# Two 128-row tiles in each step of a two-layer graph attention kernel, and the first layer's V bias moved behind the heads

## The chip, the cores and the metric

One core of one Trainium2 chip. The metric is the device time of one execution in microseconds. The kernel before took 1067.73 us, the median of three runs (1065.7 to 1071.74).

## What is computed

x is (128, 64, 384): 128 graphs of 64 nodes. Both layers are attention with 12 heads of 32, with a residual and a layer norm:

```
layer 0: q = x@Wq+bq; k = x@Wk+bk; v = x@Wv+bv          (bv not zero)
         s = q k^T / sqrt(32) + beta*adj, and -9e15 where adj <= 0
         x = layernorm(x + softmax(s) v)
layer 1: q = x@Wq.T; k = x@Wk.T; v = x@Wv.T + bv
         s = q k^T / sqrt(384) + adj; a row that is all zero gives 0
         x = layernorm(x + (softmax(s) v)@Wo.T + bo)
```

Everything is float32. The rows of a softmax sum to one, so softmax(s)(v + bv) = softmax(s) v + bv: the changed kernel uses this in layer 0.

## The kernel before

**Chunks, tiles, turns.** The 8192 rows are 16 chunks of four tiles (128 rows, two graphs, each). A turn is one chunk in one layer. `ORDER` has 32 turns: three of layer 0, then layer 1 and layer 0 by turns, at last three of layer 1. A turn has four steps, one for each tile. In a step each engine runs through a list that is written out by hand, and each engine executes its list in order; semaphores join them.

**Units.** The projections are made a chunk ahead of their use, as "units": three of q and three of k (128 output features by the 512 rows of the chunk) and four of V (128 rows by 384 features). A float32 product is split into three: each operand has a high part (rounded to fp32r) and a low part (the rest), and low x high, high x low and high x high are summed over three slices of 128, so nine matmuls a unit (L374). Units alternate between the two banks of `ps_u`; a unit waits until its bank's last user has been evicted. `units_of_step` deals the ten units of a turn over its steps: q0, k0, k1; then q1, k2; then q2, V0, V1; then V2, V3. The first of a step is "early", the others are "late".

**A step.** With `cur` the tile attended now, `prev` the one before it, `last` the one before that, and `turned` the tile two turns ahead:

- TensorE (tensor block): scores of `cur` into `ps_s` (L392, 48 matmuls of 32x64); the early unit; the result of `last` (L498: three transposes in layer 0; L374 into `ps_h`: the Wo product in layer 1); the transposes of `turned`'s rows into `ps_h` where it is of layer 1 (L410); the transposes of `prev`'s probabilities into `ps_s` (L464, six); the late units; the heads of `prev` (L486, 48 matmuls).
- VectorE: bias added to the scores (L675, two instructions), row maxima (L684; in layer 1 also of the absolute values, L683), early V eviction, the residual of `last` (z L752, then statistics), xt_lo of `turned` (L693, layer 1 only), the row sums of the exponentials (L716) and their reciprocals, late V evictions with the bias (L709), o_lo of `prev` (L733, layer 1), and at the end of a layer-0 turn the next chunk's bias (L643, L645).
- GpSimd: the maxima subtracted (`shift`, L806), bo added to `turned`'s rows (L822) or, in layer 0, its xt_lo (L832), the normalisation of `last` (L846, L852), the probabilities scaled (`scale`, L812).
- ScalarE: early eviction of a q or k unit (L585 to L591), xt_hi of `turned` (L553), the turned probabilities copied out (L559), the exponential of `cur` (L597), the late evictions, the heads copied out (L605).
- SyncE: the stores of layer 1 and the loads of x, of its transpose and of adj.

Of the kernel before, what the change touches and what calls it, by code (L numbers as in the profile page):

```python
# [12 lines left out]
P = 128  # L13
# [7 lines left out]
TILES = 4  # L21

# [15 lines left out]
Step = namedtuple("Step", "phase t cur prev last done turned units")  # L38
# [19 lines left out]

def schedule():
    steps = []  # L60
    attended = {}
    for phase in range(-1, N_TURNS + 1):
        for t in range(TILES if phase < N_TURNS else 3):
            s = TILES * phase + t
            if 0 <= phase < N_TURNS:
                attended[s] = (*ORDER[phase], t)
            turned = (*ORDER[phase + 2], t) if phase + 2 < N_TURNS else None
            units = units_of_step(phase, t) if phase < N_TURNS else []
            steps.append(Step(phase, t, attended.get(s), attended.get(s - 1), attended.get(s - 2),
                              attended.get(s - 3), turned, units))  # L70
    return steps


STEPS = schedule()

# [10 lines left out]
UNIT_ORDER = [u for s in STEPS for u in s.units]  # L86
UNIT_NO = {u: n + 1 for n, u in enumerate(UNIT_ORDER)}
QK_NO = {u: n + 1 for n, u in enumerate(u for u in UNIT_ORDER if u[2] != "v")}
V_NO = {u: n + 1 for n, u in enumerate(u for u in UNIT_ORDER if u[2] == "v")}
TURN_ORDER = [s.turned for s in STEPS if s.turned]  # L90
# [22 lines left out]
def two_gnn_layers_kernel(  # L113
# [33 lines left out]
    with ExitStack() as ctx:  # L147
# [25 lines left out]
        adj1 = [sb(f"adj1_{p}", [P, GC, NODES]) for p in range(2)]  # L173

        probs = [sb(f"probs{p}", [P, PAIRS, GT, NODES]) for p in range(2)]
        probs_t = sb("probs_t", [P, PAIRS, P])
        o_t = sb("o_t", [P, KT, P])
        o_hi = sb("o_hi", [P, KT, P], F32R)
        o_lo = sb("o_lo", [P, KT, P], F32R)
        z = [sb(f"z{p}", [P, D]) for p in range(2)]  # L180
        bv_rows = [sb(f"bv_rows{l}", [P, D]) for l in range(2)]
# [7 lines left out]
        row_max = [sb(f"row_max{p}", [P, PAIRS * GT]) for p in range(2)]  # L189
        row_abs = [sb(f"row_abs{p}", [P, PAIRS * GT]) for p in range(2)]  # L190
        row_sum = [sb(f"row_sum{p}", [P, PAIRS * GT]) for p in range(2)]
        row_inv = [sb(f"row_inv{p}", [P, PAIRS * GT]) for p in range(2)]
        row_fac = [sb(f"row_fac{p}", [P, PAIRS * GT]) for p in range(2)]
# [4 lines left out]
        w_stage = sb("w_stage", [P, KT, D])  # L198
# [8 lines left out]
        row_in = sem("row_in")  # L207
# [20 lines left out]
        xt_made = sem("xt_made")  # L228
# [16 lines left out]
        v_ready = sem("v_ready")  # L245
# [17 lines left out]
        def as_weight(home):  # L263
            flat = home[:].rearrange("p a b n -> p (a b n)") if len(home.shape) == 4 \
                else home[:].rearrange("p a n -> p (a n)")
# [3 lines left out]
                 "q1": as_weight(x1[1]), "k1": as_weight(x1[2]), "v1": as_weight(x_in[1]), "o1": w_stage[:]}  # L269
# [16 lines left out]
        def _(sp):  # L286
# [26 lines left out]
            def load_adj1(c):  # L313
                if c >= 2:
                    sp.wait_ge(biased, at((1, c - 2, TILES - 1)) + 1)
                load_adj(c, adj1[c % 2], adj1_loaded[c % 2])
# [10 lines left out]
            sp.dma_start(k_bias[:], bk0).then_inc(small_in, 16)  # L327
            sp.dma_start(beta_col[:], beta.rearrange("(o n) -> o n", o=1).partition_broadcast(P))\
# [7 lines left out]
            load_row(bv_rows[0], bv0, row_in)  # L336
# [4 lines left out]
            load_row(bv_rows[1], bv1, rows_in)  # L341
# [4 lines left out]
            for s in STEPS:  # L346
                if s.done and s.done[0] == 1:
                    _, c, t = s.done
                    sp.wait_ge(normed, at(s.done) + 1)
                    sp.dma_start(out_rows[c * CT + t * P:c * CT + (t + 1) * P, :], z[t % 2][:])\  # L350
                        .then_inc(stored[t % 2], 16)

                of = s.phase + 1
                if s.t == 0 and of < N_TURNS and ORDER[of][0] == 0 and 2 <= ORDER[of][1] < CHUNKS - 1:
                    load_xt(ORDER[of][1] + 1)
                if s.t == 1 and 0 <= s.phase < N_TURNS and ORDER[s.phase][0] == 0:
                    if ORDER[s.phase][1] < CHUNKS - 1:
                        load_adj0(ORDER[s.phase][1] + 1)
                if s.t == 2 and s.phase == 0:
                    load_x(1)  # L360
                if s.t == 2 and 1 <= s.phase <= N_TURNS and ORDER[s.phase - 1][0] == 0:
                    if ORDER[s.phase - 1][1] + 2 < CHUNKS:
                        load_x(ORDER[s.phase - 1][1] + 2)
                if s.t == 1 and 0 <= s.phase < N_TURNS - 1 and ORDER[s.phase + 1][0] == 1:
                    load_adj1(ORDER[s.phase + 1][1])
            for p in range(2):
# [3 lines left out]
        def _(pe):  # L370
# [7 lines left out]
            def scores(tile):  # L378
                layer, c, t = tile
                p = home((layer, c))  # L380
                if t == 0:
                    pe.wait_ge(qk_ready, last_qk((layer, c)))
                if at(tile) > 0:
                    pe.wait_ge(biased, at(tile))
                if at(tile) > 1:
                    pe.wait_ge(probs_t_ready, at(tile) - 1)
                for g in range(KT):
                    for b in range(GT):
                        for hh in range(HG):
# [3 lines left out]
                                ps_s[side * NODES:(side + 1) * NODES, half_of * GT + b, g * NODES:(g + 1) * NODES],  # L393
# [4 lines left out]
            def heads_read(tile):  # L398
                pe.wait_ge(o_t_ready, at(tile) + 1)
                if tile[0] == 1:  # L400
                    pe.wait_ge(o_lo_ready, second_no(tile))

            def turn_activations(tile, last_heads):
                layer, c, t = tile
                if layer == 0:
                    return
                pe.wait_ge(normed, at((0, c, t)) + 1)
                heads_read(last_heads)
                for g in range(KT):
                    last = nc.tensor.transpose(ps_h[:, 1, g * P:(g + 1) * P], x1[c % 3][:, t, g * P:(g + 1) * P],  # L410
                                               ident[:])
                last.then_inc(xt_made, 1)

            def make_unit(unit):
                layer, c, kind, n = unit
                p, no = home((layer, c)), UNIT_NO[unit]
                if no > 2:
                    freed = UNIT_ORDER[no - 3]
                    if freed[2] == "v" and freed[:2] == ORDER[-1]:
                        pe.wait_ge(last_v_copied, freed[3] + 1)  # L420
                    elif freed[2] == "v":
                        pe.wait_ge(v_ready, V_NO[freed])
                    else:
                        pe.wait_ge(qk_ready, QK_NO[freed])
# [14 lines left out]
                elif no == 1:  # L439
                    for g in range(KT):  # L440
                        pe.wait_ge(first_lo, 2 * g + 2)
                        cols = slice(n * P, (n + 1) * P)
                        nc.tensor.matmul(ps_u[:, bank, :], w_lo[w][:, g, cols], xt_hi[p][:, g, :],
                                         start=(g == 0), stop=False)
                        nc.tensor.matmul(ps_u[:, bank, :], w_hi[w][:, g, cols], xt_lo[p][:, g, :],
                                         start=False, stop=False)
                        last = nc.tensor.matmul(ps_u[:, bank, :], w_hi[w][:, g, cols], xt_hi[p][:, g, :],
# [455 lines left out]
```

## Time and profile before

| | before |
|---|---|
| median of 3 runs | 1067.73 us |
| the profiled execution's own time | 1066.61 us |
| its span | 1064.8 us |
| TensorE matmuls | 1035.8 us, 97% of the span |
| VectorE | 793.6 us, 75% |
| GpSimd | 788.6 us, 74% |
| ScalarE | 451.0 us, 42% |
| mean granted TensorE clock | 0.996 |

How to read it: PE is TensorE's matmuls, PEld its weight loads, DVE VectorE, ACT ScalarE, POOL GpSimd, SP SyncE. L374 is line 374 of the kernel. The start times in a timeline are more telling for matmuls than their lengths, since the next starts before the last has drained. `x18` is a count of instructions that follow each other.

### The profile page before, as it was taken

The page shows a single profiled execution, that of the slowest core. Times are in us where ns is not written, and L with a number is a line of the kernel's source. Part 1 is how long each engine was busy: PE and PEld are TensorE (multiplying, and loading weights), DVE is VectorE, ACT ScalarE, POOL GpSimd, SP SyncE. Part 2 cuts the span into 40 slices and gives each one's busy share as a digit, 9 for nine tenths or more (in the row PEclk, how much of TensorE's full clock was granted, in tenths as well). Part 3 has the DMA queues.
Part 4 walks back from the last instruction along what each step waited for, and adds up shares of the span by engine and source line. Part 5 has one row for each costly group of instructions (what it writes and reads, how often), then busy time and mean ns, then how long its engine had stood idle before and what let it go on. Part 6 is the DMA issues. An engine that isn't in the chain of part 4 may idle for free.

```text
span 1064.8 us, 38493 instructions
## 1 busy us (share of the span) xinstructions
PE 1035.8 (97%) x16896; PEld 898.1 (84%) x16896; DVE 793.6 (75%) x1578; ACT 451.0 (42%) x717; POOL 788.6 (74%) x646
## 2 busy tenths in 40 slices
PE   6999999999999999999999999999999999999985
PEld 5888888888888888888888888888888888888874
DVE  3587886868778687786868778687786868877884
ACT  4454434444344443444445344443434444444332
POOL 1588777778687786877778777777877867777676
PEclk9999999999999999999999999999999999999998
DMA  6421112112111121111211021121111210010100
GB/s 205 142 71 52 34 44 66 40 44 62 40 44 39 44 62 44 40 46 39 67 44 52 33 59 39 44 62 44 39 47 36 62 44 10 17 37 10 35 32 31
DMA packets 61750, 53.33 MB, mean 50 GB/s; under 512 B 35984, under 2 KB 55440, under 8 KB 61584
## 3 DMA queue, kind: packets, MB, share of 16 engines
q1 hardware_dynamic: 60752, 49.69, 15.9%
q8 instruction: 134, 2.20, 0.9%
q10 hardware_dynamic: 832, 1.18, 0.3%
q14 instruction: 32, 0.26, 0.1%
HBM read 38.28 MB, written 12.58 MB: 48 GB/s over the span
## 4 chain that ended last, share of the span: by engine, by line
PE 89%; DVE 3%; POOL 3%; issue 2%; DMA 1%; ACT 1%; POOLq 0%; SPq 0%; DVEq 0%
PE ps_u L374 53%; PE ps_h L374 9%; PE ps_s L392 8%; PE ps_s L464 8%; PE ps_h L486 7%; PE ps_h L410 2%; PE ps_h L498 2%; POOL probs L806 1%; DMA xt_in<-in_x_t 1%; DVE row_sum L716 1%; ACT probs L597 1%; DVE probs L675 1%; DVE row_max L684 1%; POOL probs L812 0%; POOL xt_lo L832 0%
## 5 line engine op out<-in xcount | busy, mean ns | idle before, releaser
L806 POOL TENSOR_TENSOR probs<-probs,row_max 128x768 f32<-128x768 f32 x128 | 193.2, 1510 | 223.2 <-DVE row_max L684 223.2
L812 POOL TENSOR_TENSOR probs<-probs,row_inv 128x768 f32<-128x768 f32 x128 | 193.2, 1509 | 2.8 <-DVE row_inv L720 2.5
L716 DVE TENSOR_REDUCE row_sum<-probs 128x12 f32<-128x768 f32 x128 | 122.0, 953 | 68.0 <-ACT probs L597 68.0
L559 ACT COPY probs_t<-ps_s 128x768 f32<-128x768 f32 x128 | 102.8, 803 | 109.9 <-PE ps_s L464 109.8
L374 PE MATMUL ps_u<-w_hi_v,xt_lo 128*128 128x384 f32 x384 | 137.7, 359 | 0.0
L374 PE MATMUL ps_u<-w_hi_v,xt_hi 128*128 128x384 f32 x384 | 129.4, 337 | 0.0
L374 PE MATMUL ps_u<-w_lo_v,xt_hi 128*128 128x384 f32 x384 | 129.1, 336 | 0.0
L684 DVE TENSOR_REDUCE row_max<-probs 128x12 f32<-128x768 f32 x128 | 121.4, 948 | 2.2
L374 PE MATMUL ps_u<-xt_hi,w_lo_q 128*128 128x512 f32 x285 | 121.6, 427 | 0.0
L597 ACT ACTIVATE probs<-probs 128x768 f32<-128x768 f32 x128 | 108.6, 849 | 28.9 <-POOL probs L806 27.0
L374 PE MATMUL ps_u<-xt_hi,w_lo_k 128*128 128x512 f32 x288 | 118.2, 410 | 0.9 <-ACT q_sb L585 0.9
L374 PE MATMUL ps_u<-xt_hi,w_hi_k 128*128 128x512 f32 x288 | 113.0, 392 | 0.0
L374 PE MATMUL ps_u<-xt_lo,w_hi_k 128*128 128x512 f32 x288 | 112.2, 390 | 0.0
L374 PE MATMUL ps_u<-xt_lo,w_hi_q 128*128 128x512 f32 x285 | 111.8, 392 | 0.0
L374 PE MATMUL ps_u<-xt_hi,w_hi_q 128*128 128x512 f32 x285 | 111.8, 392 | 0.0
L852 POOL TENSOR_SCALAR x<-z,mean_var,rstd 128x384 f32<-128x384 f32 x64 | 106.1, 1658 | 6.7
L852 POOL TENSOR_SCALAR z<-z,mean_var,rstd 128x384 f32<-128x384 f32 x64 | 105.9, 1655 | 6.7
L486 PEld LDWEIGHTS ps_h<-probs_t,v_sb 64*32 64x32 f32 x6144 | 72.3, 105 | 41.8 <-issue 40.6
L464 PE MATMUL ps_s<-ident,probs 128*128 128x128 f32 x768 | 105.9, 274 | 1.2 <-DVE probs L675 1.1
L392 PE MATMUL ps_s<-k_sb,q_sb 32*64 32x64 f32 x6144 | 99.8, 231 | 1.2 <-ACT k_sb L587 0.8
L486 PE MATMUL ps_h<-probs_t,v_sb 64*32 64x64 f32 x6144 | 92.6, 223 | 2.5 <-DVE xt_lo L693 1.4
L392 PEld LDWEIGHTS ps_s<-k_sb,q_sb 32*64 32x64 f32 x6144 | 82.2, 131 | 13.6 <-ACT k_sb L587 1.2
(80 smaller groups left out, 2102.6 us busy)
## 6 DMA issues: line engine op xcount, KB each, us to landing
x_in<-in_x SPq DMA_DIRECT2D x16, 768.0 KB, 4.6
out<-z SPq DMA_DIRECT2D x64, 192.0 KB, 1.9
xt_in<-in_x_t SPq DMA_DIRECT2D x15, 768.0 KB, 4.7
adj<-in_adj SPq DMA_DIRECT2D x64, 128.0 KB, 3.0
xt_in<-in_x_t SPq DMA_DIRECT2D x3, 256.0 KB, 4.4
q_sb<-in_wq ACTq DMA_DIRECT2D x3, 192.0 KB, 4.6
k_sb<-in_wk ACTq DMA_DIRECT2D x1, 576.0 KB, 7.4
v_sb<-in_wv SPq DMA_DIRECT2D x1, 576.0 KB, 7.3
```

The lines of the kernel that those rows point to most:

```text
L374: last = nc.tensor.matmul(dst, a(g), b(g), start=(g == 0 and n == 0), stop=(g == KT - 1 and n == 2))
L392: last = nc.tensor.matmul(ps_s[side * NODES:(side + 1) * NODES, half_of * GT + b, g * NODES:(g + 1) * NODES], q_sb[p][rows, g, GT * t + b, :],
L410: last = nc.tensor.transpose(ps_h[:, 1, g * P:(g + 1) * P], x1[c % 3][:, t, g * P:(g + 1) * P], ident[:])
L464: last = nc.tensor.transpose(ps_s[:, i // KT, (i % KT) * P:(i % KT + 1) * P], probs[t % 2][:, i, :, :], ident[:])
L486: last = nc.tensor.matmul(ps_h[hh * HD:(hh + 1) * HD, b, g * NODES:(g + 1) * NODES], v_sb[p][keys, t, h * HD:(h + 1) * HD], probs_t[keys, ...
L559: nc.scalar.copy(probs_t[:].rearrange("p (a i) n -> p a (i n)", a=2), ps_s[:, 0:2, 0:KT * P]).then_inc(probs_t_ready, 1)
L597: nc.scalar.activation(e, e, ACT.Exp).then_inc(exp_ready, 1)
L684: nc.vector.tensor_reduce(row_max[t % 2][:], rows, AX_X, ALU.max).then_inc(max_ready, 1)
L716: nc.vector.reduce_sum(row_sum[p][:], probs[p][:].rearrange("p i b k -> p (i b) k"), AX_X)\
L806: nc.gpsimd.tensor_tensor(s, s, over_keys(row_max[p]), ALU.subtract).then_inc(shifted, 1)
L812: nc.gpsimd.tensor_tensor(s, s, over_keys(row_inv[p]), ALU.mult).then_inc(probs_ready, 1)
L852: nc.gpsimd.tensor_scalar(dst, z[t % 2][:], mean_var[t % 2][:, 0:1], rstd[t % 2][:], ALU.subtract, ALU.mult).then_inc(normed, 1)
```

## The change

Turns 2 to 27 have two steps of two tiles; turns 0, 1 and 28 to 31 keep four steps of one. In a paired step each engine takes both tiles: TensorE the scores of both one behind the other, then one early unit, both results, both tiles' columns, both turned probabilities, four late units, both heads. `cur`, `prev` and `last` are now tuples, so in a paired turn `last` is the pair two steps back, which belongs to the turn before. Four buffers of probabilities (and of row maxima, sums and so on) take the place of two, two of turned probabilities the place of one; `o_t`, `o_hi` and `o_lo` hold two tiles.

The transposes of layer 1's rows ("x" units, `columns`) go through the banks of `ps_u`, between the early and the late units, so that both banks of `ps_h` serve results.

Layer 0's V is copied out by ScalarE with no bias; its bias is added when the heads are copied out, as a column, in three ScalarE instructions a step. Layer 1's V stays on VectorE.

At the start TensorE runs ten products on the identity; the first two units are made together, slice by slice, high parts first. The first scores wait for each slice's q and k alone. SyncE's stores stand behind the step's loads, one step earlier than before. Wo is staged in the space of `adj1`, whose first load therefore waits for Wo's low part. The bias of V in layer 0 is loaded as a column beside the other small constants.

The core of the diff (`j` is the place of a tile in its step):

```diff
+def slots(phase):
+    if 2 <= phase <= N_TURNS - 5:
+        return [(0, 1), (2, 3)]
+    return [(0,), (1,), (2,), (3,)] if phase < N_TURNS else [(0,), (1,)]
...
+def columns(s):
+    return [(*tile[:2], "x", tile[2]) for tile in s.turned if tile[0] == 1]
...
+UNIT_ORDER = [u for s in STEPS for u in early(s) + columns(s) + late(s)]
...
         # TensorE
+            warm_up()
+            first_units()
             for s in STEPS:
-                if s.cur:
-                    scores(s.cur)
+                for j, tile in enumerate(s.cur):
+                    scores(tile, j, s)
                 for unit in early(s):
...
+                for j, tile in enumerate(s.last):
+                    result(tile, j, s)
+                for unit in columns(s):
+                    turn_activations(unit)
+                for j, tile in enumerate(s.prev):
+                    turn_probs(tile, j, s)
                 for unit in late(s):
...
+                for j, tile in enumerate(s.prev):
+                    heads(tile, j, s)
...
         # ScalarE
             def unit_out(unit):
-                if kind == "v" and (layer, c) != ORDER[-1]:
+                if kind == "v" and layer == 1 and (layer, c) != ORDER[-1]:
                     return
...
+            def heads_out(tiles):
...
+                if layer == 1:
+                    nc.scalar.copy(dst, src).then_inc(o_t_ready, len(tiles))
+                    return
+                for g in range(KT):
+                    done = nc.scalar.activation(dst[:, g::KT, :, :], src[:, g::KT, :, :], ACT.Identity,
+                                                bias=bv_col[:, g:g + 1])
+                done.then_inc(o_t_ready, len(tiles))
...
+                for unit in early(s):
+                    unit_out(unit)
...
+                for j, tile in enumerate(s.prev):
+                    probs_out(tile, j, s)
+                for tile in s.cur[:1]:
+                    exponentials(tile)
+                for unit in late(s)[:1]:
                     unit_out(unit)
+                for tile in s.cur[1:]:
+                    exponentials(tile)
+                for unit in late(s)[1:]:
+                    unit_out(unit)
...
         # VectorE
+                for j, tile in enumerate(s.cur):
+                    add_bias(tile, j, s)
+                for tile in s.cur[:1]:
+                    maxima(tile)
...
+                if s.phase >= 0:
+                    for tile in s.turned:
+                        activations_lo(tile)
+                for j in range(2):
+                    for tile in s.last[j:j + 1]:
+                        residual(tile, j)
+                    if len(s.ts) == 2:
+                        for unit in late(s)[j:j + 1]:
+                            unit_out(unit)
+                for tile in s.cur[1:]:
+                    maxima(tile)
+                for tile in s.cur[:1]:
+                    sums(tile)
+                for unit in late(s)[2 if len(s.ts) == 2 else 0:]:
+                    unit_out(unit)
+                for tile in s.cur[1:]:
+                    sums(tile)
...
         # GpSimd
+                for tile in s.cur[:1]:
+                    shift(tile)
...
+                for tile in s.cur[1:]:
+                    shift(tile)
+                for j in range(2):
+                    for tile in s.last[j:j + 1]:
+                        inverse_deviation(tile)
+                        normalise(tile)
+                    for tile in s.cur[j:j + 1]:
+                        scale(tile)
```

## Rows read from the trace of the kernel before

**Rows 1.** the page's first part: busy us (share of the span) x instructions of each engine.

```profile
span 1064.8 us, 38493 instructions
...
PE 1035.8 (97%) x16896; PEld 898.1 (84%) x16896; DVE 793.6 (75%) x1578; ACT 451.0 (42%) x717; POOL 788.6 (74%) x646
```

**Rows 2.** the chain of waits: start in us, length, engine, tile, line, count.

```profile
430.72 3.13 PE ps_u L374 x18
...
495.09 3.13 PE ps_u L374 x18
```

**Rows 3.** timeline of TensorE, one layer-0 step: start us, length us, engine, line.

```profile
501.51 0.82 PE L464 MATMUL ps_s<-ident,probs 128*128 128x128 f32 x6
...
502.08 0.42 PE L374 MATMUL ps_u<-w_hi_v,xt_lo 128*128 128x384 f32 x1
...
503.40 0.34 PE L374 MATMUL ps_u<-w_lo_v,xt_hi 128*128 128x384 f32 x1
...
503.58 0.34 PE L374 MATMUL ps_u<-w_hi_v,xt_hi 128*128 128x384 f32 x1
503.85 0.56 PEld L486 LDWEIGHTS ps_h<-probs_t,v_sb 64*32 64x32 f32 x48 [0.26 <-issue]
...
504.51 0.78 PE L392 MATMUL ps_s<-k_sb,q_sb 32*64 32x64 f32 x48
...
505.22 0.50 PE L374 MATMUL ps_u<-xt_hi,w_lo_q 128*128 128x512 f32 x1
...
505.78 0.40 PE L374 MATMUL ps_u<-xt_hi,w_hi_q 128*128 128x512 f32 x1
...
507.40 0.49 PE L498 MATMUL ps_h<-ident,o_t 128*128 128x128 f32 x3
```

**Rows 4.** timeline of the other engines, the end of that turn and one layer-1 step.

```profile
505.23 0.49 DVE L709 TENSOR_TENSOR v_sb<-ps_u,bv_rows 128x384 f32<-128x384 f32 x1
...
505.64 0.41 DVE L643 TENSOR_SCALAR bias<-adj 128x512 f32<-128x512 f32 x1
...
506.76 1.01 DVE L675 TENSOR_TENSOR probs<-ps_s,adj 128x384 f32<-128x384 f32 x2
...
507.81 0.95 DVE L683 TENSOR_REDUCE row_abs<-probs 128x12 f32<-128x768 f32 x1
...
509.54 0.55 DVE L752 TENSOR_TENSOR z<-ps_h,x_in 128x384 f32<-128x384 f32 x1
...
509.70 1.48 POOL L806 TENSOR_TENSOR probs<-probs,row_max 128x768 f32<-128x768 f32 x1 [1.53 <-DVE row_max L684]
...
511.07 0.55 DVE L693 TENSOR_TENSOR xt_lo<-ps_h,xt_hi 128x384 fp32r<-128x384 f32 x1
511.13 1.02 POOL L822 TENSOR_TENSOR x<-x,bo_rows 128x384 f32<-128x384 f32 x1
511.21 0.85 ACT L597 ACTIVATE probs<-probs 128x768 f32<-128x768 f32 x1 [1.27 <-POOL probs L806]
...
511.96 0.67 ACT L587 ACTIVATE k_sb<-ps_u,k_bias 128x512 f32<-128x512 f32 x1
512.09 0.95 DVE L716 TENSOR_REDUCE row_sum<-probs 128x12 f32<-128x768 f32 x1 [0.47 <-ACT probs L597]
512.11 0.56 POOL L846 TENSOR_TENSOR rstd<-var_eps,minus_half 128x1 f32<-128x1 f32 x1
...
512.77 1.66 POOL L852 TENSOR_SCALAR x<-z,mean_var,rstd 128x384 f32<-128x384 f32 x1
```

**Rows 5.** timeline of TensorE's start: its first unit and the first scores.

```profile
6.52 0.77 PE L443 MATMUL ps_u<-xt_hi,w_lo_q 128*128 128x512 f32 x1 [6.52 <-DVE w_lo_q L654]
...
23.20 0.78 PE L392 MATMUL ps_s<-k_sb,q_sb 32*64 32x64 f32 x48 [0.78 <-ACT k_sb L587]
```

**Rows 6.** windows in the tail: stretch, length, busy of each engine, granted clock.

```profile
1024.00:1028.00 4.00, 2.35 (x102) 1.86 (x100) 2.83 (x9) 1.85 (x4) 3.80 (x4) 1.00 0.03 6
1028.00:1032.00 4.00, 3.91 (x16) 3.85 (x17) 3.53 (x6) 0.00 (x0) 3.19 (x3) 0.57 0.14 49
```

More of the change, by code:

```diff
@@ L36 @@
 FIRST_AT = [[0, 1], [2, 3], [4, 5], []]
-Step = namedtuple("Step", "phase t cur prev last done turned units")
+Step = namedtuple("Step", "phase ts cur prev last turned units")
 def at(tile):
@@ L83, in late @@
     return s.units[len(early(s)):]
-UNIT_ORDER = [u for s in STEPS for u in s.units]
+UNIT_ORDER = [u for s in STEPS for u in early(s) + columns(s) + late(s)]
 UNIT_NO = {u: n + 1 for n, u in enumerate(UNIT_ORDER)}
-QK_NO = {u: n + 1 for n, u in enumerate(u for u in UNIT_ORDER if u[2] != "v")}
-V_NO = {u: n + 1 for n, u in enumerate(u for u in UNIT_ORDER if u[2] == "v")}
-TURN_ORDER = [s.turned for s in STEPS if s.turned]
+QK_NO = {u: n + 1 for n, u in enumerate(u for u in UNIT_ORDER if u[2] in "qk")}
+V_NO = {u: n + 1 for l in range(2) for n, u in enumerate(u for u in UNIT_ORDER if u[2] == "v" and u[0] == l)}
+TURN_ORDER = [tile for s in STEPS for tile in s.turned]
 TURN_NO = {x: n + 1 for n, x in enumerate(TURN_ORDER)}
@@ L438, in make_unit @@
                         lambda g: w_lo[w][:, g, :])
[L439 to L447, printed above, removed]
-                                                start=False, stop=(g == KT - 1))
                 else:
@@ L471, in heads @@
                 pe.wait_ge(probs_t_ready, at(tile) + 1)
-                if at(tile) > 0:
-                    pe.wait_ge(z_ready, at(tile))
-                if turned and turned[0] == 1:
-                    pe.wait_ge(xt_lo_ready[1], low_no(turned))
+                if s.last:
+                    pe.wait_ge(z_ready, at(s.last[-1]) + 1)
                 if (layer, c) == ORDER[-1]:
@@ L708, in unit_out @@
                     dve.wait_ge(heads_made, at((*user, TILES - 1)) + 1)
[L709 to L710 removed]
+                nc.vector.tensor_tensor(v_sb[p][:, n, :], ps_u[:, (UNIT_NO[unit] - 1) % 2, 0:D], bv_rows[:],
+                                        ALU.add).then_inc(v_ready[1], 1)
             def sums(tile):
[L713 to L714 removed]
+                layer, c, p = tile
                 dve.wait_ge(exp_ready, at(tile) + 1)
@@ L777, in _ @@
                     unit_out(unit)
-                if s.last:
-                    residual(s.last)
-                if s.turned and s.phase >= 0:
-                    activations_lo(s.turned)
-                if s.cur:
-                    sums(s.cur)
-                for unit in late(s):
-                    unit_out(unit)
+                if s.phase >= 0:
+                    for tile in s.turned:
+                        activations_lo(tile)
[10 more added lines that the diff above has]
+                for unit in late(s)[2 if len(s.ts) == 2 else 0:]:
+                    unit_out(unit)
+                for tile in s.cur[1:]:
+                    sums(tile)
+                if len(s.ts) == 2:
+                    for t in s.ts:
+                        if (s.phase, t) in w_lo_at:
+                            weights_lo(w_lo_at[s.phase, t])
                 if s.prev:
                     heads_lo(s.prev)
-                if s.t == 3 and s.cur and s.cur[0] == 0 and s.cur[1] < CHUNKS - 1:
-                    make_bias0(s.cur[1] + 1)
+                if 3 in s.ts and s.cur and s.cur[0][0] == 0 and s.cur[0][1] < CHUNKS - 1:
+                    make_bias0(s.cur[0][1] + 1)
         @block.gpsimd
@@ L840, in last_v @@
                 pool.wait_ge(last_v_copied, n + 1)
-                nc.gpsimd.tensor_tensor(rows, rows, bv_rows[layer][:], ALU.add).then_inc(last_v_ready, 1)
+                nc.gpsimd.tensor_tensor(rows, rows, bv_rows[:], ALU.add).then_inc(last_v_ready, 1)
             def inverse_deviation(tile):
```

328 lines of the change are left out of this document (165 added, 163 removed).

## The prediction

> **What bounds the kernel now.** First the page's busy shares: TensorE is busy 1035.8 us of a span of 1064.8, VectorE and GpSimd about three quarters, ScalarE 42% [rows 1]. Then the chain of waits: from one layer-1 turn to the next it repeats every 64.37 us, and nearly all of it is TensorE [rows 2]. The reader is to see there a kernel in which the other engines are hidden, thus one that gains only by less TensorE time, and loses as soon as one of the others falls behind TensorE. The chip's own time of this execution was 1066.61 us, 1.8 around the span and 1.1 below the median of the three runs; I sum on 1066.6.
>
> **What pairing gives TensorE.** The timeline's start times show what a change of matmul kind costs [rows 3]. 48 head products take 504.51 - 503.85 = 0.66 us though their weight loads are issued within 0.56; 48 scores take 505.22 - 504.51 = 0.71. So about 0.1 us of each is the drain ahead of the next kind, and a second tile behind the first saves it: 2 x 0.1. The first unit after the scores starts a further 0.1 late (2.18 us to L498, against 9 x 0.23 = 2.08), the last unit ahead of the heads leaves 0.27 rather than 0.18, and the unit after the turned probabilities starts slowly: together 0.3. That is 0.5 us a pair (between 0.2, the drains alone, and 0.6), with four pairs in each 64.37: 2.1 us in two turns, 27 us in the 26 paired turns.
>
> **Do the others keep up?** Everything below is from the start of a pair's scores. TensorE's pieces, from [rows 3]: scores of two 1.3; early unit 2.2; results of two layer-0 tiles 0.6 (three transposes each, at the rate of six in 502.08 - 501.51 = 0.57), of two layer-1 tiles 2 x 1.57 = 3.15 (nine products 0.175 apart); columns of two tiles 0.6; turned probabilities of two 1.15; a late q or k unit 2.07, a late V unit 1.57; heads of two 1.2. In pairs `last` is always the turn before, so a layer-1 turn (13 of the 26) holds layer-0 results, the columns and layer-0 units; a layer-0 turn holds layer-1 results and layer-1 units. If nothing waits, the layer-1 turn's pairs last 15.7 and 13.5 us, the layer-0 turn's 17.5 and 15.5: 62.2.
>
> Now VectorE in a layer-1 turn, whose order is written out: two bias additions, maxima of the first tile, two xt_lo, two residuals, and only then the maxima of the second. By [rows 4]: start at 1.4; biases 2 x 1.02 to 3.45; maxima (two reductions, 507.81 to 509.70 less a gap) 1.85 to 5.3; xt_lo 2 x 0.55 to 6.4; residuals 2 x 1.55 (509.54 to 511.07) to 9.5; maxima of the second 1.85 to 11.35. GpSimd's shift (1.48, and 0.08 ahead of it) ends at 12.9, the exponential (0.85) at 13.8.
>
> ScalarE's order in the pair is: exponential A, late unit 1, **exponential B, late units 2 to 4**. There are two unit banks, so the fourth late unit needs the bank of the second, and the second is evicted only behind exponential B. In the second pair (late units V0 to V3, with layer 0's now on ScalarE) V1 leaves at 14.3 (0.5 us; a 128x384 copy on ScalarE isn't in the rows, VectorE's takes 0.49, the exponential of twice the size 0.85, and I keep both ends). V3 could have started at 5.85 + 0.1 + 3 x 1.57 = 10.6. TensorE waits 3.75 us in order; the pair lasts 14.35 + 1.75 + 1.2 = 17.3 instead of 13.5.
>
> The first pair starts with a debt. In the second pair of the layer-0 turn, VectorE waits for V0 (made at 7.8 + 1.67 + 0.2 = 9.65) between the residuals: V0 0.54, residual, V1, maxima end at 13.25; shift 14.8, exponential 15.65, sums (0.95 and 0.25) 16.9, and the next chunk's bias (505.64 to 506.76, 1.1) 18.1 [rows 4]. That pair lasts 15.5, so the next one's biases start at 2.65 rather than 1.4. GpSimd is later still: shift 14.8, two normalisations of 2.3 and two scalings of 1.5 end at 22.4, which is 6.9 in the next pair, whose second turned tile TensorE wanted at 5.3. This wait of 1.6 us is swallowed by the later one: shift B 14.15, exponential 15.05, k1 evicted (0.67) 15.7, fourth unit and heads: 19.2 instead of 15.7.
>
> In the layer-0 turn's first pair the same order does no harm: there are no abs-maxima and no xt_lo on VectorE, exponential B ends at 11.9, before its second late unit is made (12.1). In its second pair VectorE evicts V. They last 17.5 and 15.5. Sum: 17.3 + 19.2 + 17.5 + 15.5 = 69.5 against 64.37, so 5.1 us for two turns, 13 times: **+67 us**. Without the debt it would be 68.3, +51 us.
>
> The clock. The tail shows what idle time does: in the four microseconds from 1024 TensorE was busy 2.35 us, and in the next four its granted clock was 0.57 (part of them at 1.2 GHz, the rest at 2.4) [rows 6]. That is 0.43 x 4 = 1.7 us lost. The wait of 3.75 us is longer than that one. I take half of 13 such waits: +11 us; the ends are 0 and 26 x 1.7 = 44.
>
> The Trainium skill ("TensorE: Matmul & The Clock Gate", Part 1: The HAM clock gate) says that the clock follows how busy the engine has just been. By this rule, and by the rows at 1024 us which agree, the wait costs more than its length; had it no such effect the sum would end 11 us lower. The same page (Architectural detail: the array is 16× 32×32) gives ScalarE, VectorE and GpSimd strictly ordered queues; it speaks against this change, since a ready eviction can't pass the exponential ahead of it, and the order of ScalarE's instructions at 511.21 and 511.96 doesn't contradict it.
>
> **The other edits.** Layer 0's V on ScalarE takes 0.54 us from VectorE four times in a layer-1 turn, where VectorE's chain would be longer with it; it is in the chain above. Layer 0's heads leave in three ScalarE instructions of 256 columns; a line through 768 columns in 0.85 and 512 in 0.67 gives 0.49 each, 1.5 us; the results want them 3.5 us into the next pair, so nothing (with that cover gone 0.7). Columns through the unit banks: the first late unit needs the first xt_lo, ready at 5.85 when TensorE comes at 5.95: nothing, at most 0.5 a pair. SyncE's loads now stand ahead of its stores; a load's waits there were met a turn earlier, and a z buffer is wanted again a whole pair later: nothing. One small load more at the start (about 0.5) is behind GpSimd's and ScalarE's work. wo staged in the adjacency buffer delays a load wanted a turn later: nothing. The start: before, TensorE begins at 6.52 and the first scores at 23.20 [rows 5]; the two first units now start on their high parts and share each piece as it lands, with ten products on the identity ahead. This ends them some 3 us earlier, but k0 needs its low weights and k2's bank needs ScalarE behind four copies: -2 us (0 to -4). The last turns stay single: 0.
>
> 1066.6 + 67 + 11 - 2 = **1142 us**.
>
> **Rivals.** (1) The pairing pays in full: no wait, 1066.6 - 27 - 2 = 1037 us. For it: TensorE is saturated, and the others have a quarter of their time free. Against: that share doesn't set when exponential B ends. It decides the other way once exponential B ends before about 10 us in a layer-1 pair, and VectorE's work ahead of it alone ends at 11.35. (2) The wait is there, but short: no debt, no fall of the clock, the start at its best: 1066.6 + 51 - 4 = 1113 us. For it: every piece is measured alone, and small overlaps (the k eviction at 511.96 starts before the exponential of 511.21 + 0.85 ends) add up. (3) The clock falls at each wait of both pairs: 1066.6 + 67 + 44 - 2 = 1176 us. For it: a wait of 2 us did it in the tail; against: there it followed small matmuls, here full ones.
>
> **Chances.** Forecast 0.57, rival 1 0.1, rival 2 0.15, rival 3 0.15, 0.03 for a mixture that ends within half a per cent. 0.5% is about what a measurement here can tell from no change. The range runs from rival 2 to rival 3, 1112 to 1176, and leaves rival 1 out. Faster 0.1, same 0.03, slower 0.87.
>
> **What would show it.** In the profile after: TensorE's busy share falls to about 92%; waits of TensorE at ps_u for ScalarE's evictions, 26 of them, about 3.7 us in the second pair and 2 to 3 in the first of each layer-1 turn, none in layer-0 turns; ScalarE idle ahead of the exponential, released by GpSimd's shift, and this by the maxima; the granted clock below 1 in some of these stretches; the period 69 to 72 us; first scores near 21. I am wrong if TensorE shows no wait on ps_u there, or if V1 is evicted before exponential B.

## The result, and the profile after

The changed kernel took 1173.8 us, the median of four runs, against 1067.2 before (four runs). One of the four, of 1288.8 us at a granted clock of 0.743, was disturbed and is left out of what follows: the other three took 1166.64, 1171.57 and 1176.04, which is 1.0969 times as long as before, 95% interval 1.0935 to 1.1003. The execution profiled took 1176.04 us. The forecast was 1142 and its range 1112 to 1176. The direction and the wait that was forecast held; the time lies near the upper end of the range because the clock cost more than forecast and because one cause, waits for instructions, was missing from the sum.

The page of the changed kernel, against [rows 1]:

```profile
span 1174.2 us, 38335 instructions
...
PE 1046.7 (89%) x16916; PEld 913.5 (78%) x16916; DVE 768.8 (65%) x1488; ACT 479.6 (41%) x805; POOL 790.7 (67%) x646
```

Five repeats of a layer-1 and a layer-0 turn, cut at the start of the first biases (stretch, length, busy of PE, PEld, DVE, ACT, POOL with the count of instructions, granted clock, share of the DMA engines, GB/s), against the 64.37 us of [rows 2]:

```profile
414.67:483.58 68.91, 62.62 (x1055) 54.77 (x1054) 47.47 (x94) 29.02 (x48) 49.06 (x41) 1.00 0.16 44
483.58:560.68 77.10, 66.26 (x1052) 57.74 (x1051) 47.60 (x93) 29.02 (x48) 49.10 (x41) 0.93 0.15 40
560.68:630.15 69.47, 64.76 (x1066) 56.93 (x1066) 47.43 (x93) 28.96 (x48) 49.06 (x41) 1.00 0.16 44
630.15:701.11 70.96, 62.70 (x1049) 54.71 (x1048) 47.43 (x94) 29.02 (x48) 49.06 (x41) 0.98 0.16 43
701.11:778.97 77.86, 67.97 (x1063) 59.28 (x1062) 47.62 (x93) 29.00 (x48) 49.11 (x41) 0.96 0.14 39
```

The reader is to see two kinds of repeat: 69 to 71 us with the clock near 1, as forecast (69.5), and 77 to 78 with the clock at 0.93 to 0.96. The clock isn't all that sets them apart: each of the two long ones also holds four waits in the middle of the scores, 5.3 and 5.4 us together, the short ones none or one. What TensorE waited for (total us, times, longest):

```profile
PE ps_u L389 <- ACT v_sb L606: 37.1, 13, 3.2
PE ps_s L409 <- issue: 29.0, 20, 2.2
PE ps_u L389 <- ACT k_sb L623: 23.3, 14, 2.1
PE ps_h L389 <- DVE o_lo L783: 11.3, 8, 2.4
PE ps_s L496 <- POOL probs L877: 6.5, 8, 0.8
PE ps_s L496 <- DVE probs L723: 5.7, 9, 1.0
```

The first and the third are the forecast waits: a unit that can't have its bank until ScalarE has evicted V1, or k1. The fourth was there before, in the tail (10.3 us in 8). The second was not forecast: TensorE stops in the middle of the scores (L409), with no semaphore behind it.

One second pair of a layer-1 turn, whose scores start at 430.62 (timeline: start, length):

```profile
430.62 1.28 PE L409 MATMUL ps_s<-k_sb,q_sb 32*64 32x64 f32 x96
...
431.94 1.95 DVE L723 TENSOR_TENSOR probs<-ps_s,adj_both 128x384 f32<-128x384 f32 x4 [3.96 <-PE ps_s L409]
...
437.64 0.86 ACT L633 ACTIVATE probs<-probs 128x768 f32<-128x768 f32 x1
...
438.50 0.48 ACT L606 COPY v_sb<-ps_u 128x384 f32<-128x384 f32 x1
...
440.62 0.94 DVE L735 TENSOR_REDUCE row_max<-probs 128x12 f32<-128x768 f32 x1
...
441.64 1.47 POOL L871 TENSOR_TENSOR probs<-probs,row_max 128x768 f32<-128x768 f32 x1 [2.53 <-DVE row_max L735]
...
443.14 0.84 ACT L633 ACTIVATE probs<-probs 128x768 f32<-128x768 f32 x1 [4.16 <-POOL probs L871]
...
443.89 0.84 ACT L606 COPY v_sb<-ps_u 128x384 f32<-128x384 f32 x2
...
444.40 0.44 PE L389 MATMUL ps_u<-w_hi_v,xt_lo 128*128 128x384 f32 x1 [2.82 <-ACT v_sb L606]
```

This is the forecast chain, link by link: exponential A and V0 in time; then ScalarE is idle for 4.16 us, until the second maxima (end 441.56) and the shift are done; then exponential B, and V1 only behind it. V3 starts 13.8 us after the scores; forecast 14.35.

### The profile page after: what moved, and what is told of

It is laid out like the page before. It is cut to its first block, busy times and chain, and to the rows that moved or that the text cites. A ratio compares the mean times of both kernels' runs of the same rounds, so it can differ in the third digit from the quotient of the medians.

```text
span 1174.2 us, 38335 instructions
## 1 busy us (share of the span) xinstructions
PE 1046.7 (89%) x16916; PEld 913.5 (78%) x16916; DVE 768.8 (65%) x1488; ACT 479.6 (41%) x805; POOL 790.7 (67%) x646
## 4 chain that ended last, share of the span: by engine, by line
PE 56%; DVE 22%; POOL 8%; issue 7%; ACT 5%; DMA 2%; DVEq 0%; POOLq 0%; SPq 0%
PE ps_u L389 32%; PE ps_h L389 8%; POOL probs L871 6%; PE ps_s L409 5%; PE ps_h L516 5%; DVE row_max L735 4%; PE ps_s L496 4%; ACT probs L633 3%; DVE stats L804 3%; DVE z L802 3%; DVE probs L723 2%; DVE row_abs L734 2%; DVE xt_lo L745 2%; DMA xt_in<-in_x_t 2%; DVE row_sum L765 1%
## 5 line engine op out<-in xcount | busy, mean ns | idle before, releaser
L389 PE MATMUL ps_u<-w_hi_v,xt_lo 128*128 128x384 f32 x384 | 138.1, 360 | 37.5 <-ACT v_sb L606 37.1
L595 ACT COPY probs_t<-ps_s 128x768 f32<-128x768 f32 x128 | 98.4, 803 | 108.7 <-PE ps_s L496 108.1
L389 PE MATMUL ps_u<-xt_hi,w_lo_k 128*128 128x512 f32 x288 | 117.2, 407 | 24.3 <-ACT k_sb L623 23.3
L389 PE MATMUL ps_u<-w_hi_v,xt_hi 128*128 128x384 f32 x384 | 132.9, 346 | 0.0
L389 PE MATMUL ps_u<-w_lo_v,xt_hi 128*128 128x384 f32 x384 | 132.8, 346 | 0.0
L409 PE MATMUL ps_s<-k_sb,q_sb 32*64 32x64 f32 x6144 | 91.5, 236 | 29.8 <-issue 29.0
L389 PE MATMUL ps_u<-xt_lo,w_hi_q 128*128 128x512 f32 x282 | 114.5, 406 | 0.2 <-issue 0.2
L389 PE MATMUL ps_u<-xt_hi,w_hi_q 128*128 128x512 f32 x282 | 114.3, 405 | 0.0
L496 PE MATMUL ps_s<-ident,probs 128*128 128x128 f32 x768 | 99.4, 275 | 12.2 <-POOL probs L877 6.5
L783 DVE TENSOR_TENSOR o_lo<-ps_h,o_hi 128x768 fp32r<-128x768 f32 (+1 forms) x38 | 31.5, 829 | 119.6 <-ACT o_hi L643 119.6
L409 PEld LDWEIGHTS ps_s<-k_sb,q_sb 32*64 32x64 f32 x6144 | 78.1, 134 | 40.5 <-issue 33.1
L389 PEld LDWEIGHTS ps_u<-w_hi_v,xt_lo 128*128 128x128 f32 x384 | 74.6, 194 | 42.2 <-ACT v_sb L606 41.3
```

What stands on the lines that cost most here:

```text
L389: last = nc.tensor.matmul(dst, a(g), b(g), start=(g == 0 and n == 0), stop=(g == KT - 1 and n == 2))
L409: last = nc.tensor.matmul(ps_s[side * NODES:(side + 1) * NODES, half_of * GT + b, (j * KT + g) * NODES:(j * KT + g + 1) * NODES], q_sb[p][ ...
L496: last = nc.tensor.transpose(ps_s[:, 2 * j + i // KT, (i % KT) * P:(i % KT + 1) * P], probs[t][:, i, :, :], ident[:])
L595: nc.scalar.copy(probs_t[j][:].rearrange("p (a i) n -> p a (i n)", a=2), ps_s[:, 2 * j:2 * j + 2, 0:KT * P]).then_inc(probs_t_ready, 1)
```

## The experiments

**Two evictions ahead of exponential B.**

```diff
                 for tile in s.cur[:1]:
                     exponentials(tile)
-                for unit in late(s)[:1]:
+                for unit in late(s)[:2]:
                     unit_out(unit)
                 for tile in s.cur[1:]:
                     exponentials(tile)
-                for unit in late(s)[1:]:
+                for unit in late(s)[2:]:
                     unit_out(unit)
```

> The changed kernel, but in a paired step ScalarE evicts the first two late units ahead of the second tile's exponential, not one. Theory (order of ScalarE): TensorE's 26 long waits at ps_u (13 of 2.1 and 13 of 3.2 us, 68 us together) go; what they covered comes out, above all the wait for the second tile's scaled probabilities after the layer-0 turn (about 1.5 us, 13 times). 1095 to 1115 us. Rival (the whole chain of VectorE and GpSimd is too long for the pair, ScalarE's order is only where it shows): the wait moves to the turned probabilities, and the time stays above 1150 us.

1109.59 us, 1.0393 of before (1.0347 to 1.0439). The waits for V and k evictions are gone from the list; the theory holds, the rival is out. The turned probabilities still wait (6.8 us for GpSimd and 5.5 us for VectorE), and the waits inside the scores grew:

```profile
PE ps_s L409 <- issue: 36.4, 20, 3.0
```

**Layer 0's V on VectorE.** VectorE's `unit_out` takes layer 0 with a `tensor_copy`, ScalarE's skips it.

> The changed kernel, but layer 0's V is evicted by VectorE (a plain copy, the bias still comes with the heads). Theory (order of ScalarE): in the second pair of a layer-1 turn V1 no longer stands behind the exponential, so 13 waits of 3.2 us go; the 13 of 2.1 us in the first pair stay, since they are q and k units. Less 1 us a turn for the longer chain on VectorE: about 1140 us. Rival (VectorE is the bound of a layer-1 turn): its four copies of 0.5 us make the turn longer, 1165 us or more.

1153.29 us, 1.0784 (1.0732 to 1.0836). The 13 waits behind V1 went, the 13 behind k1 stayed (21.8 us), as the theory says, but the gain was some 20 us (1.0969 to 1.0784 of before) where the expectation had 34 (1173.8 to 1140): the waits inside the scores rose from 29.0 to 39.9 us.

**The heads ahead of the last late unit.**

```diff
+                held = late(s)[-1:] if len(s.ts) == 2 and s.prev else []
-                for unit in late(s):
+                for unit in late(s)[:len(late(s)) - len(held)]:
                     if UNIT_NO[unit] > 2:
                         make_unit(unit)
                 for j, tile in enumerate(s.prev):
                     heads(tile, j, s)
+                for unit in held:
+                    make_unit(unit)
```

> The changed kernel, but in a paired step TensorE makes the heads ahead of the last late unit, so 96 head products no longer stand next to 96 scores; ScalarE copies the heads out ahead of that unit's eviction. It adds one change of matmul kind a pair (0.3 us, 52 times, +15 us). Theory (instruction supply: TensorE runs through 384 instructions in 2.4 us and its next block of instructions isn't there; the waits inside the scores come 512 instructions apart): the waits of 1.5 to 2.5 us inside the scores go, about 18 of them, -33 us; together 1150 to 1162 us. Rival (those waits are a semaphore's or a memory conflict with the other engines at the turn of a pair): they stay, 1180 to 1190 us.

1108.47 us, 1.0367 (1.0327 to 1.0406): a miss to the good side, 42 us below the expected range. Of the waits inside the scores, 1.3 us in four are left; the rival is out. The rest I hadn't seen: the heads now fill part of the time in which the last unit waits for its bank, so these waits fell from 60.4 (37.1 and 23.3) to 31.4 us (21.8 and 9.6), and the granted clock rose from 0.968 to 0.989.

```profile
PE ps_u L389 <- ACT v_sb L609: 21.8, 13, 2.0
PE ps_s L496 <- DVE probs L729: 11.5, 14, 1.0
PE ps_u L389 <- ACT k_sb L626: 9.6, 14, 0.7
```

**The second maxima ahead of the residuals**, on top of the first experiment.

```diff
+                for tile in s.cur[1:]:
+                    maxima(tile)
                 for j in range(2):
                     for tile in s.last[j:j + 1]:
                         residual(tile, j)
...
-                for tile in s.cur[1:]:
-                    maxima(tile)
                 for tile in s.cur[:1]:
                     sums(tile)
```

> As the first kernel of this set, and VectorE finds the second tile's maxima right behind xt_lo, ahead of both residuals, in a paired step. Theory (the order on VectorE makes exponential B late, and the debt after the layer-0 turn): no wait at ps_u nor at the turned probabilities is left; what is left are the waits inside the scores, 18 to 26 of 1.8 us. 1037 us from the pairing alone plus 33 to 47: 1070 to 1085 us, thus no gain over the kernel before. Rival: the debt has another source, no better than the first kernel of this set (within 5 us).

1101.1 us, 1.0304 (1.0265 to 1.0343). The waits of order are gone, but for one of 1.0 us at the turned probabilities. What the change adds to the list is now waits that no semaphore ends:

```profile
PE ps_s L409 <- issue: 39.1, 20, 4.3
PE ps_u L389 <- issue: 6.0, 3, 3.6
```

Two of the three at `ps_u` (3.6 and 2.1 us) are of the same kind as those in the scores: they stand at the same places in the program, as counted below.

This kernel has turns in which nothing waits. The scores of the first pair of a layer-1 turn, one repeat apart in the chain of waits:

```profile
386.79 1.21 PE ps_s L409 x72
...
448.68 1.21 PE ps_s L409 x72
```

61.89 us against 64.37, both at a granted clock of 1.00: 2.5 us a repeat, forecast 2.1. It is the pairing's own, since the version with single tiles and all other edits (the last one below) repeats every 64.37 us as well. The total missed the expectation by 16 us all the same; the granted clock was 0.977, which over this span is 21 us more than 0.996 by the estimate of share times span. The rival (within 5 us of the first kernel of the set) is out by the list of waits rather than by the time: 1101.1 is 8.5 us below 1109.59.

**Shifting the program by 64 instructions.** `WARM_UP = 26` in place of 10 in that kernel.

> The kernel with two evictions first and the maxima early, and 26 products on the identity at the start in place of 10: 64 instructions more on TensorE, so all that follows stands 64 further in its block. Theory (instruction supply): the waits inside the scores stay about 20 of 2 us, but in other steps: the three between 112 and 146 us of that kernel go, and the first come at the pairs that there stood at 246, 261 and 275 us. The time is that kernel's plus 2 to 4 us at the start. Rival (a cause in the data or the other engines): the same steps wait as before.

1098.76 us, one run, too few to judge the time; the theory is about places. TensorE's part of both timelines at the same two places; first the kernel with `WARM_UP = 10`, whose scores at 245.74 run through:

```profile
245.74 1.28 PE L409 MATMUL ps_s<-k_sb,q_sb 32*64 32x64 f32 x96
...
261.31 1.28 PE L409 MATMUL ps_s<-k_sb,q_sb 32*64 32x64 f32 x96
```

and with 26:

```profile
243.95 1.12 PE L409 MATMUL ps_s<-k_sb,q_sb 32*64 32x64 f32 x81
246.48 0.37 PE L409 MATMUL ps_s<-k_sb,q_sb 32*64 32x64 f32 x15 [1.40 <-issue]
...
261.12 1.05 PE L409 MATMUL ps_s<-k_sb,q_sb 32*64 32x64 f32 x72
263.68 0.46 PE L409 MATMUL ps_s<-k_sb,q_sb 32*64 32x64 f32 x24 [1.50 <-issue]
...
277.99 0.91 PE L409 MATMUL ps_s<-k_sb,q_sb 32*64 32x64 f32 x64
281.90 0.69 PE L409 MATMUL ps_s<-k_sb,q_sb 32*64 32x64 f32 x32 [3.00 <-issue]
```

The waits came at the three foretold pairs, whose work is unchanged. Of the three that should have gone, one went and two shrank (start to start from 2.0 to 1.0 and from 3.4 to 1.5 us). So the cause lies in the place in the program. Counted through the trace, all 20 waits inside scores of the changed kernel stand after 193 (or, with one record missing, 194) plus a whole number of times 256 of TensorE's recorded instructions, and within a group of waits they are 512 apart. With everything shifted by 64 instructions all 19 stand at 193 or 194 plus a multiple of 256 again, now at other work. The page's third part has 134 packets with 2.20 MB on the instruction queue, 16.4 KB each.

These packets have times in the trace, which show what TensorE waits for. There is one packet to each such place. In all 20 waits TensorE goes on 1.1 to 1.6 us after the end of the packet that comes next ahead of that place, and nowhere in the trace does it pass a place sooner than 1.1 us after that end. In 18 of the 20 the packet had started 0.7 to 1.3 us after TensorE passed the place before, and it took 0.9 to 1.7 us. From one place to the next that makes 3.1 to 4.1 us, and TensorE had run through the 256 instructions between in 1.5 to 2.2 us. In the kernel before, every packet had ended at least 3.1 us before TensorE came to its place. The Trainium skill ("Runtime: NRT & Kernel Launch", Instruction fetch mechanics) gives blocks of 16 KiB, 256 instructions, which this count confirms; its remark that the fetch is hidden because instructions are issued more slowly than they arrive does not hold here, with 29.0 us of such waits.

**The heads held back only where a block ends** and **in all pairs**, both with the two orders mended.

```diff
+HELD_AT = {(2 + k // 2, 2 * (k % 2))
+           for k in [1, 2, 3, 12, 13, 14, 15, 22, 23, 24, 25, 27, 33, 34, 35, 36, 44, 45, 46, 47]}
-                held = late(s)[-1:] if len(s.ts) == 2 and s.prev else []
+                held = late(s)[-1:] if (s.phase, s.ts[0]) in HELD_AT else []
```

> Both orders mended: ScalarE evicts two late units ahead of the second exponential, VectorE finds the second maxima ahead of the residuals, and in every paired step TensorE makes the heads ahead of the last late unit. Theory (three waits of the change, all of order, and the pairing's own gain of 27 us behind them): no wait in the scores, at ps_u or at the turned probabilities; 1037 us plus one more change of kind a pair (52 x 0.3 = 15): 1048 to 1058 us, the first version below the kernel before. Rival (the pairing has no gain of its own, or the lower clock belongs to it): 1066 us or more.

> As the kernel with both orders mended, but the heads go ahead of the last late unit in only 20 of the 52 paired steps: those before scores in which a block of 256 instructions ends 98 or more instructions behind the first of them, which is where the waits stood in the trace of the kernel with two evictions first and the maxima early (19 of them, and one of 0.8 us). Theory (instruction supply, by place in the program): no wait inside any scores, and 32 x 0.3 = 10 us less than with all 52 changed: 1038 to 1048 us. Rival (the waits depend on time or on other engines, and move to other steps): some 10 to 20 waits of 2 us come back elsewhere, 1065 us or more.

All pairs: 1095.44 us, 1.0252 (1.021 to 1.0295). Where a block ends: 1077.47, 1.0081 (1.0052 to 1.011). Both missed by 30 to 40 us, and both times lie where the rivals had put them (1066 us or more, 1065 or more), but not for the rivals' reasons: the pairing's gain is there (61.89 us above), and in the second kernel the waits did not move, all five of 1.7 to 2.6 us in its scores stand at places where the kernel with the two orders mended waited too. The waits inside the scores fell from 39.1 to 12.0 and 12.1 us, but did not go: a unit of nine products gives the block some 1.7 us more, and where it comes later than that TensorE still waits, 1.9 to 2.8 us start to start behind the loads of x. There its packet starts 2.6 to 3.3 us after the place before. With all pairs changed a second cost appears:

```profile
PE ps_s L496 <- DVE probs L729: 12.7, 14, 1.0
PE ps_s L409 <- issue: 12.0, 9, 2.4
PE ps_u L389 <- DVE xt_lo L751: 7.7, 13, 0.6
```

In the second pair of a layer-0 turn the held unit is V3; it is made 1.2 us later, VectorE evicts it, takes the sums and the next chunk's bias later, and the next pair's biases and xt_lo are late; this chain is read from the lists, no run tests it. What the clock (0.986 and 0.987) adds to both is about 10 us, an estimate.

**The load of x one pair later.** SyncE's `load_x` moves behind the stores of the next pair.

> The kernel with two evictions first and the maxima early; SyncE issues each load of x (768 KB) not in the second pair of the layer-1 turn but one pair later, behind that pair's stores. In that kernel the waits inside the first scores of a layer-0 turn were the longest (3.4, 3.0, 4.6, 3.4, 3.5 us, the others 1.5 to 2.3), right after the load of x and four loads of adj were issued. Theory (TensorE's instruction block queues behind these loads on the same DMA engines): those five fall to 1.5 to 2.8 us, and the kernel gains 5 to 8 us. Rival (their length has nothing to do with the loads): they stay over 3 us.

1096.49 us (two runs, 1092.83 and 1100.16; 1.0276, 1.0243 to 1.031). The kernel with the early load, then with the late one (SyncE's issue and TensorE's scores; the view with 485.55 ends six products early):

```profile
476.32 0.39 SPq L305 DMA_DIRECT2D x_in<-in_x  x1
...
480.05 1.16 PE L409 MATMUL ps_s<-k_sb,q_sb 32*64 32x64 f32 x83
485.55 0.40 PE L409 MATMUL ps_s<-k_sb,q_sb 32*64 32x64 f32 x7 [4.34 <-issue]
...
503.86 0.95 PE L409 MATMUL ps_s<-k_sb,q_sb 32*64 32x64 f32 x68
506.13 0.48 PE L409 MATMUL ps_s<-k_sb,q_sb 32*64 32x64 f32 x28 [1.33 <-issue]
```

```profile
472.70 1.16 PE L411 MATMUL ps_s<-k_sb,q_sb 32*64 32x64 f32 x83
475.31 0.36 PE L411 MATMUL ps_s<-k_sb,q_sb 32*64 32x64 f32 x13 [1.45 <-issue]
...
489.90 0.43 SPq L305 DMA_DIRECT2D x_in<-in_x  x1
...
491.79 0.95 PE L411 MATMUL ps_s<-k_sb,q_sb 32*64 32x64 f32 x68
496.27 0.72 PE L411 MATMUL ps_s<-k_sb,q_sb 32*64 32x64 f32 x28 [3.53 <-issue]
```

The long wait moved with the load. Start to start, the 3.4, 4.6, 3.4 and 3.5 us in first pairs of layer-0 turns became 1.4 to 1.7, the fifth (3.0) went, and 1.6 to 1.9 us in four other pairs became 3.4 to 4.4. The packets of the instruction queue show why: ahead of the five long waits (3.0 to 4.6 us) of the kernel with the early load they start 1.9 to 3.3 us after TensorE passed the place before, ahead of the others at most 1.6 us, and they take 1.3 us against 0.9 to 1.2. So the block is carried hardly more slowly, its transfer begins later; that it stands behind the load on the same DMA engines remains the likely reason, not a shown one. Nothing is gained, since another wait grows instead; two runs are too few to judge the part of the expectation on the total.

**Pairs in the layer-0 turns only.** `slots` gets `and ORDER[phase][0] == 0`; all orders as in the changed kernel.

> The changed kernel with pairs in the layer-0 turns only; layer-1 turns keep single tiles, all orders as in the changed kernel. Theory (ScalarE's order hurts only where VectorE also has abs-maxima and xt_lo): no wait at ps_u; half of the pairing's gain, 14 us; of heads and scores never more than 288 instructions stand together, so the waits inside the scores are few and under 1 us. 1050 to 1062 us. Rival (pairs hurt in both kinds of turn): 1090 us or more.

1063.42 us, 0.9956 (0.9936 to 0.9976), 1.4 us above what was expected. No wait for V or k evictions, four in the scores with 2.2 us together (the longest 1.1, expected under 1), clock 0.997.

**The same with the second maxima early**, and two evictions first.

> Pairs in the layer-0 turns only, and in them the second maxima ahead of the residuals; two late units evicted ahead of the second exponential. In the trace with pairs in the layer-0 turns TensorE still waited 0.9 us for VectorE's biases ahead of the turned probabilities, once in each of the 13 pairs of turns, since the maxima of the second tile stand behind the V evictions there. Theory: these waits go, 13 x 0.9 = 11 us: 1050 to 1056 us. Rival (the lateness is the next chunk's bias and the sums, whatever the order of the maxima): within 3 us of 1063.

1059.7 us, 0.9936 (0.9921 to 0.995), the fastest, and 3.7 us above the expected range. The expectation had read the waits for VectorE's biases wrongly: of the 13, twelve are of 0.26 to 0.27 us and one is of 1.0, 4.2 us together and not 11. They went to 1.0 in one, and the first step of a layer-1 turn, where they stood, lasts 10.58 us in place of 11.02 where nothing else disturbs it. The intervals of the two overlap: that these 3.7 us are a gain is likely, not shown. In both traces the heads of the layer-1 turn's second tile now start 0.5 us late, 13 times (6.7 us), which I didn't take further.

**Single tiles everywhere**, with all other edits of the change: `slots` without its pairs.

> The changed kernel with single tiles in every turn: all its other edits stay (start, columns through the unit banks, layer 0's V on ScalarE and its bias behind the heads, order of SyncE). Theory (everything the change costs comes from the pairs): 1062 to 1067 us, 0 to 4 us below the kernel before, by the earlier start; no wait at ps_u, none in the scores. Rival (one of the other edits costs something of its own): 1072 us or more.

1063.76 us, 0.9966 (0.9951 to 0.9981), as expected: the other edits together bring 3.6 us (1066.66 x 0.0034), and the whole loss is the pairs'. Pairs in the layer-0 turns alone are within this kernel's interval, so a gain from them isn't shown; with the maxima early they lie 4 us below it, and the intervals (to 0.995, from 0.9951) just don't overlap.

## Why the prediction was right, and where it was not

- **TensorE's own gain.** Forecast 27 us in 26 turns; measured 2.48 x 13 = 32. The drains and first-matmul delays read from the start times of [rows 3] were a little more than I took.
- **The wait behind exponential B.** The mechanism is shown: moving one eviction removed it. Its size was right too. One repeat of the changed kernel has neither a wait in the scores nor a fall of the clock; here are its four pairs (from scores to scores), then a first pair of a layer-1 turn with a wait of 1.79 us in its scores:

```profile
411.10:430.62 19.52, 16.29 (x267) 13.03 (x262) 15.31 (x28) 8.59 (x15) 16.82 (x14) 1.00 0.21 63
430.62:447.34 16.72, 13.90 (x267) 12.64 (x262) 12.04 (x24) 7.57 (x14) 11.48 (x10) 1.00 0.33 81
447.34:464.62 17.28, 17.28 (x273) 15.02 (x267) 9.78 (x19) 7.66 (x12) 14.06 (x13) 1.00 0.04 14
464.62:480.01 15.39, 15.39 (x275) 14.54 (x268) 10.33 (x21) 5.21 (x8) 6.70 (x7) 1.00 0.05 15
557.11:576.60 19.49, 16.22 (x268) 13.20 (x262) 15.30 (x28) 8.54 (x15) 16.80 (x14) 1.00 0.20 62
```

Forecast 19.2, 17.3, 17.5 and 15.5 us. The repeat is 68.91 us, 7.02 above the 61.89 without waits: 91 us in 13, and the gross price in my sum was 67 + 27 = 94. The list of waits has less (60.4 us at ps_u, 12.2 at the turned probabilities) because a wait in the scores hides some of it, as the last line shows: TensorE comes later to the turned probabilities, doesn't wait there, and the pair lasts as long as without. The debt from the layer-0 turn was real: the wait at the turned probabilities is gone with the maxima early.

- **The step that was missing.** "Scores of two 1.3" and "heads of two 1.2" took the issue rate of 48 products [rows 3] for 96 and 96 in a row, and the sum put the supply of instructions at nothing. Doubling both puts 384 instructions into 2.4 us, and the next instruction block isn't there: 29.0 us in 20 waits. Nothing in the trace of before shows such a wait; there 192 instructions stood together, less than a block.
- **The clock.** Forecast 11 us, half of the 13 long waits. The mean clock went from 0.996 to 0.968; 0.032 x 1174 less 0.004 x 1065 is 33 us, an estimate and on the high side, since clock that is lost while TensorE waits costs nothing. It falls also behind the waits inside the scores. An example from the changed kernel, before, in and after one fall:

```profile
511.00:514.50 3.50, 1.17 (x7) 0.85 (x5) 2.65 (x5) 0.77 (x2) 2.17 (x3) 0.96 1.01 285
514.50:521.00 6.50, 6.01 (x187) 5.40 (x188) 1.60 (x4) 2.09 (x5) 6.40 (x5) 0.50 0.28 43
521.00:528.00 7.00, 6.31 (x63) 5.70 (x54) 5.14 (x11) 1.41 (x3) 2.83 (x4) 0.99 0.01 4
```

TensorE was busy a third of the first stretch, and ran at 1.2 GHz for the next 6.5 us. The rule that I had weighed, that of the Trainium skill ("TensorE: Matmul & The Clock Gate", Part 1: The HAM clock gate), agrees; I had given it too few waits. Without a wait in the scores it fell too: the pair from 207.67 to 226.55 us has one wait, of 3.2 us, a granted clock of 0.85 and 18.88 us, against 16.72 us for the same pair above, with a wait of 2.8 us and a clock of 1.00.

- **The sum again.** 1064.8 - 32 + 91 - 4 = 1120 us is the span with the waits of order alone; the forecast, without its 11 us for the clock, had some 1130. The other 54 us up to 1174 are the waits for instructions and the clock together, forecast at 11. Their two estimates, 29.0 and 33, make 62: they overlap with each other and with the waits of order, and no run parts them.
- **What was luck.** The forecast missed a cause of some 20 to 30 us and sized the clock at a third or half of what it cost; its order terms were 10 us too high. That the time still lies in the range comes from the range's upper end, which a rival with another reason had set.
- **The other edits** were priced at -2 us, measured -3.6. The first scores came at 20.67 us, 2.5 earlier than in [rows 5].
- **Rivals.** The first, pairing in full, is out for the changed kernel. None of the versions with pairs in all 26 turns reached it: mending the orders uncovered the instruction supply each time. The second, a wait without debt and without a fall of the clock, is out: the first pair lasted 19.5 us, where without debt it would be 18, and the clock fell. The third, a clock that falls at every wait, came nearest in time, but it counted no wait for instructions, and the clock did not fall at every wait (1.00 in the pairs above).

## What to carry to other kernels

Where an engine's list is written out by hand, look for the instruction that stands behind the longest chain of the others, and put what is already ready ahead of it; here one eviction moved past one exponential was worth some 62 us (1.0969 to 1.0393 of before). Before putting two runs of very small matmuls side by side, count instructions as well as time: a saving of 0.1 us a drain was paid for with waits of 1.5 to 4.5 us. Waits and clock don't add up one for one: a wait of 3 us can also cost clock in the work behind it, and a wait ahead of a longer one can cost nothing. So the price of an order is better read from repeats with and without it than from the list of waits.

## What the runs showed of the hardware

- TensorE went through 384 small products and weight loads in 2.4 us and then mostly waited 1.4 to 2.5 us (start to start), at places fixed in the program, a multiple of 256 instructions apart. It went on 1.1 to 1.6 us after a packet of 16384 bytes on the instruction queue had ended.
- With a load of 768 KB issued in the pair before, that packet started 1.9 to 3.3 us after the place before in place of about 1 us, and the wait was 3.0 to 4.6 us.
- With 192 and 192 in a row, split by a unit of 1.7 us, the idle times in the scores were at most about half a microsecond, except behind such a load (1.9 to 2.8 us start to start).
- With at most 288 in a row (pairs in the layer-0 turns) four such waits were left, 2.2 us together.
- The granted clock was lowest where TensorE waited most: 0.968 where it was not busy for 127 us of the span, 0.997 with pairs in the layer-0 turns only (37 us). Idle time alone doesn't set it: 73 us with the heads ahead of the last unit, nearly none of it in the scores, went with 0.989, and 69 us with both orders mended and 39.1 us of it in the scores with 0.977.
